# Attention and mixture-of-experts block: row order, a second gate bank, earlier scatters, later weight loads, one unused tile moved, and inner rows loaded by ScalarE

## The reference

```
xt = layernorm(x)                               # 2048 x 512
scores = softmax(xt @ Wg.T)                     # 16 experts
topi = 4 experts a token, out of the 2 best groups of 4
h = silu(xt @ W1[e].T) * (xt @ W3[e].T)         # 352 inner values, expert e
y = sum over the 4 experts of score * (h @ W2[e].T)
z = silu(xt @ Ws1.T) * (xt @ Ws3.T) @ Ws2.T     # shared part, 704 inner values
out = x + y + z
```

## Time and profile before

| | |
|---|---|
| time, median of 3 runs | 955.37 us (953.28 to 955.61) |
| profiled execution's own time | 954.32 us |
| its span | 952.7 us |
| PE busy | 914.0 us (96%) |
| DVE, ACT, POOL busy | 557.2, 332.3, 494.8 us |
| moved by DMA | 218.97 MB |

### The profile page before, as it was taken

The page is one execution under the profiler, slowest core; times in us unless marked ns, Lnnn a source line. Parts: engine busy times, 40 slices in busy tenths (PEclk is TensorE's granted clock), DMA queues, the critical chain, the costliest instruction groups (busy, mean ns, idle before and its releaser), DMA issues.

```text
span 952.7 us, 19359 instructions
## 1 busy us (share of the span) xinstructions
PE 914.0 (96%) x4962; PEld 811.7 (85%) x4963; DVE 557.2 (58%) x1103; ACT 332.3 (35%) x708; POOL 494.8 (52%) x346
## 2 busy tenths in 40 slices
PE   8999998899999996899999999999999999997998
PEld 5778876688889985899999999999999999896997
DVE  6656766898885542344444444444444444465997
ACT  4466553443334221233333333333333333321221
POOL 1137777772276675044644665456666634046771
PEclk9999999999999999899999999999999999998999
DMA  6739995664677767657785777777778755577884
GB/s 210 259 116 388 390 402 183 238 201 139 194 268 243 249 221 229 203 154 247 218 260 165 248 247 248 245 246 231 248 247 255 246 166 154 155 212 209 265 264 131
DMA packets 180649, 218.97 MB, mean 230 GB/s; under 512 B 56576, under 2 KB 124160, under 8 KB 180224
## 3 DMA queue, kind: packets, MB, share of 16 engines
q1 hardware_dynamic: 118080, 123.49, 40.4%
q0 software_dynamic: 20816, 79.44, 24.9%
q10 hardware_dynamic: 41712, 15.54, 6.0%
HBM read 127.38 MB, written 91.03 MB: 229 GB/s over the span
## 4 chain that ended last, share of the span: by engine, by line
PE 75%; DVE 9%; issue 5%; DMA 5%; ACT 3%; SPq 1%; POOL 1%; ACTq 0%; DVEq 0%; POOLq 0%
PE ps L1153 14%; PE ps L1154 14%; PE ps L1155 14%; PE ps L1205 8%; PE ps L1207 8%; PE ps L1206 8%; DMA hblk<-h_d 2%; PE ps L1008 2%; PE ps L1021 2%; DVE st L1450 1%; PE ps L955 1%; DVE res L1448 1%; SPq L408 1%; DMA xslot_d<-scat,sloti 1%; DVE st L1267 1%
## 5 line engine op out<-in xcount | busy, mean ns | idle before, releaser
L1153 PE MATMUL ps<-whi,xhi 128*128 (+1 forms) x888 | 291.3, 328 | 10.7 <-issue 8.6
L1154 PE MATMUL ps<-wlo,xhi 128*128 (+1 forms) x888 | 288.7, 325 | 0.0
L1155 PE MATMUL ps<-whi,xlo 128*128 (+1 forms) x888 | 288.6, 325 | 0.0
L1153 PEld LDWEIGHTS ps<-whi,xhi 128*128 128x128 f32 x888 | 169.3, 191 | 17.4 <-issue 12.7
L1525 DVE TENSOR_TENSOR hrow<-ps,sg 128x352 f32<-128x352 f32 x95 | 49.8, 524 | 224.6 <-ACT sg L827 224.4
L1154 PEld LDWEIGHTS ps<-wlo,xhi 128*128 128x128 f32 x888 | 169.5, 191 | 4.0
L1155 PEld LDWEIGHTS ps<-whi,xlo 128*128 128x128 f32 x888 | 169.0, 190 | 0.0
L827 ACT ACTIVATE sg<-ps 128x352 f32<-128x352 f32 x111 | 51.5, 464 | 283.9 <-PE ps L1155 283.9
L834 ACT ACTIVATE xhi<-ps 128x512 fp32r<-128x512 f32 x112 | 66.9, 597 | 150.7 <-DVE ps L1486 150.6
L560 POOL TENSOR_TENSOR wlo<-raw,whi 128x2816 fp32r<-128x2816 f32 x16 | 100.5, 6283 | 2.4 <-POOL whi L558 0.3
L654 POOL DMA_INDIRECT raw<-yslot_d,sloti x64 | 69.3, 1083 | 57.7 <-DMA yslot_d<-ysb 28.3
(11 more groups left out here) (199 smaller groups left out, 1597.7 us busy)
## 6 DMA issues: line engine op xcount, KB each, us to landing
raw<-wexp_in POOLq DMA_DIRECT2D x18, 2176.0 KB, 11.4
xslot_d<-zero SPq DMA_DIRECT2D x10, 2048.0 KB, 21.2
xg<-xslot_d SPq DMA_DIRECT2D x320, 64.0 KB, 2.1
yslot_d<-ysb SPq DMA_DIRECT2D x80, 256.0 KB, 2.2
h_d<-hrow ACTq DMA_DIRECT2D x79, 192.0 KB, 2.5
hblk<-h_d SPq DMA_DIRECT2D x79, 192.0 KB, 2.6
xg<-xn_d SPq DMA_DIRECT2D x128, 64.0 KB, 3.4
xq<-x_in SPq DMA_DIRECT2D x16, 256.0 KB, 3.4
```

Source lines behind the costliest of these rows:

```text
L1153: pe.matmul(ps[:, 2 + m, 0:INTER], xh, wh, start=(k == 0), stop=False)
L1154: pe.matmul(ps[:, 2 + m, 0:INTER], xh, wl, start=False, stop=False)
L1155: mm = pe.matmul(ps[:, 2 + m, 0:INTER], xl, wh, start=False, stop=(k == KT - 1))
```

## The change

Six things are changed, all in the second half.

1. Row order: DVE multiplies expert tile 0 (`first_row`) ahead of the last shared tile's addition instead of behind it.
2. Bank 7: an odd expert tile's gate half goes to bank 7. `up` of an expert tile starts its gate half when the silu of the tile two before is done, and waits for the tile before only ahead of the multiplier half.
3. Scatter: token tile t is scattered when `up` of tile t-1 is done, not of tile t+1 (both cut off at the ends).
4. Weight sets: the raw load of set o+1 is issued inside `split` of set o, once set o's own raw weights have landed, not right behind the split of set o-1.
5. Unused tile: the table that counts leading tiles is read two entries earlier, so there is one leading tile less (2 instead of 3 with these inputs) and one trailing tile more. The odd tiles get a count of their own for the first gather.
6. `load_h` goes from SP's program to ACT's, behind `store_h` of the tile after.

```diff
+        def gate_bank(base, p):
+            return 7 if base == NT and p else 2
...
-            def load_h(t, r, turn):
-                if type(t) is int and t == NR - 1:
-                    return
-                hold(sp, h_stored[r], 16 * (turn + 1))
-                if type(t) is not int or t >= XG:
-                    hold(sp, h_tr, NT + t - XG + 1)
-                sp.dma_start(hblk[:, r, :], h_d[r * P:(r + 1) * P, :]).then_inc(h_loaded[r], 16)
-
             sp.wait_ge(y_zeroed, 16 * (NR - NT * TOPK) // 8)
-            stream(sp, [(NR, True, [(-1, load_h), (XG + 1, load_slots), (-3, store_y)], None),
-                        (NT, False, [(0, None), (XG + 1, load_tile(NT + NR, xn_d)), (-4, store_out)], None)], XG)
+            stream(sp, [(NR, True, [(XG + 1, load_slots), (-3, store_y)], None),
+                        (NT, False, [(XG + 1, load_tile(NT + NR, xn_d)), (-4, store_out)], None)], XG)
...
                 hold(pool, raw_loaded[p], 16 * (half + 1))
+                if type(o) is not int or 2 < o < NW - 1:
+                    next_raw(o + 1, 1 - p)
                 hold(pool, mm1, 2 + before)
...
             def next_raw(o, p):
-                hold(pool, w13_ready, o + 1)
-                hold(pool, w2_ready, o + 1)
-                pool.dma_start(raw[:, p, :].rearrange("p (c n) -> p c n", c=PIECES), wexp[bass.ds(o + 2, 1), :, :, :].rearrange("a c p n -> p (a c) n")).then_inc(raw_loaded[p], 16)
+                hold(pool, w13_ready, o - 1)
+                hold(pool, w2_ready, o - 1)
+                pool.dma_start(raw[:, p, :].rearrange("p (c n) -> p c n", c=PIECES), wexp[bass.ds(o, 1), :, :, :].rearrange("a c p n -> p (a c) n")).then_inc(raw_loaded[p], 16)
...
-                pool.wait_ge(mm1, 2 + (min(t + 2, NT) if t else 1))
+                pool.wait_ge(mm1, 2 + max(t, 1))
...
-            def set_and_next(o, p, half):
-                split(o + 2, p, half + 1, tiles_through(o + 2))
-                if type(o) is int and o == 0:
-                    pool.wait_ge(first_lo, 2 * NT)
-                    load_weights(1, 3)
-                next_raw(o + 2, p)
-
-            pipeline(pool, NW - 4, [(0, set_and_next)])
-            for o in range(NW - 2, NW):
-                split(o, o % 2, o // 2, tiles_through(o))
+            def set_on(t, p, half):
+                split(t + 3, 1 - p, half + 1 + p, tiles_through(t + 3))
+
+            split(2, 0, 1, tiles_through(2))
+            pool.wait_ge(first_lo, 2 * NT)
+            load_weights(1, 3)
+            pipeline(pool, NW - 4, [(0, set_on)])
+            split(NW - 1, (NW - 1) % 2, (NW - 1) // 2, tiles_through(NW - 1))
 
 
             pool.wait_ge(w2_ready, NW)
-            stored = pool.value_load(order[0:1, NRP + E:NRP + E + 1], min_val=8 * NT * TOPK, max_val=16 * (NR // 2))
-            for p in range(2):
+            for p, at in enumerate((NRP + E, NTAB - 1)):
+                stored = pool.value_load(order[0:1, at:at + 1], min_val=8 * NT * TOPK, max_val=16 * (NR // 2))
                 hold(pool, y_stored[p], stored)
...
+            def load_h(t, r, turn):
+                if type(t) is int and t == NR - 1:
+                    return
+                hold(act, h_stored[r], 16 * (turn + 1))
+                if type(t) is not int or t >= XG:
+                    hold(act, h_tr, NT + t - XG + 1)
+                act.dma_start(hblk[:, r, :], h_d[r * P:(r + 1) * P, :]).then_inc(h_loaded[r], 16)
...
-            stream(act, [(NR, True, [(0, by_two(silu_g(NT))), (0, store_h), (-2, high_first), (2, by_two(x_high_e)), (-2, high_later), (-3, by_two(y_evac))], None),
...
+            stream(act, [(NR, True, [(0, by_two(silu_g(NT))), (0, store_h), (-1, load_h), (-2, high_first), (2, by_two(x_high_e)), (-2, high_later), (-3, by_two(y_evac))], None),
...
-                    two = base == NT and type(t) is int and t in (2, 3)
                     pe.wait_ge(x_lo, base + t + 1)
-                    if 1 in halves and not two:
+                    if base == NT:
+                        pe.wait_ge(silu, base + t - 1 if type(t) is not int or t else base)
+                    elif 1 in halves:
                         pe.wait_ge(h_ready, base + t)
                     else:
                         pe.wait_ge(silu, base + t)
@@ -1142,17 +1147,18 @@
                         return
                     pe.wait_ge(w13_ready, need)
                     for m in halves:
-                        if two and m:
+                        if base == NT and m:
                             pe.wait_ge(h_ready, base + t)
+                        bank = 3 if m else gate_bank(base, p)
...
-                            pe.matmul(ps[:, 2 + m, 0:INTER], xh, wh, start=(k == 0), stop=False)
-                            pe.matmul(ps[:, 2 + m, 0:INTER], xh, wl, start=False, stop=False)
-                            mm = pe.matmul(ps[:, 2 + m, 0:INTER], xl, wh, start=False, stop=(k == KT - 1))
+                            pe.matmul(ps[:, bank, 0:INTER], xh, wh, start=(k == 0), stop=False)
+                            pe.matmul(ps[:, bank, 0:INTER], xh, wl, start=False, stop=False)
+                            mm = pe.matmul(ps[:, bank, 0:INTER], xl, wh, start=False, stop=(k == KT - 1))
...
-                step(dve.tensor_scalar(total[:, 1, 0:NL], const[:, C_TILE + NT * TOPK + 1:C_TILE + NT * TOPK + 2 * NL:2], total[:, 0, 0:1], None, ALU.is_ge))
+                step(dve.tensor_scalar(total[:, 1, 0:NL], const[:, C_TILE + NT * TOPK - 1:C_TILE + NT * TOPK - 2 + 2 * NL:2], total[:, 0, 0:1], None, ALU.is_ge))
...
+                step(dve.tensor_scalar(ecmp[:, 0:NR // 2, 0], const[0:1, C_TILE + 1:C_TILE + NR:2], ntile[0:1, 0, E - 1:E], 16.0, ALU.is_lt, ALU.mult))
+                step(dve.tensor_reduce(tabf[:, NRP + E + 1 + NL:NTAB], ecmp[:, 0:NR // 2, 0], AX, ALU.add))
...
+            def first_row(t, r, turn):
+                if type(t) is int and t == NT - 1:
+                    h_row(NT)(0, 0, 0)
+
+            def later_rows(t, r, turn):
+                if type(t) is not int or t >= 1:
+                    h_row(NT)(t, r, turn)
+
+            pipeline(dve, NT, [(2, x_turn_on), (1, x_low_on), (0, h_mult_on), (0, route_1), (0, route_2), (-1, first_row), (-1, add_shared(0)), (0, h_low_on),
                                (0, second_set), (0, expert_rows)], ramp=11, ring=XG)
-            stream(dve, [(NR, True, [(0, h_row(NT)), (-2, turn_first), (-2, low_first), (2, x_turn_r), (-2, turn_later), (2, x_low_r), (-2, low_later),
+            stream(dve, [(NR, True, [(0, later_rows), (-2, turn_first), (-2, low_first), (2, x_turn_r), (-2, turn_later), (2, x_low_r), (-2, low_later),
```

More of the change, by code:

```diff
@@ L39 @@
 NRP = NR + 4
+NTAB = NRP + E + 1 + NL + 1
 PIECE = WCOL // NT
```

9 lines of the change are left out of this document (4 added, 5 removed).

## The result

| | before | after |
|---|---|---|
| median of the runs, us | 954.33 (951.97 to 955.61, 4 runs) | 941.78 (939.81 to 943.77, 4 runs) |
| profiled execution, us | 954.32 | 943.77 |
| its span, us | 952.7 | 942.2 |

The account below looks back on a forecast made before the run. PE's matmuls were taken to bound the experts at 5.97 us a tile, leaving only stalls to win: 954.3 - 12.7 (start) - 8.8 (end) + 2.5 (steady) = 935.3, or 936.4 on the median's side; 8-in-10 range 929.5 to 944.

Parts of the forecast that it names:

- Start: Shared stage to experts, 350 to 400 us: 17.7 us lost, 5 left, gain 12.7; bounds 1 and 12 left.
- The gate: Scatters released by an earlier up: they end near 343 instead of 353.8 and land 10.8 us earlier.
- the leading tile's cover: At the start, the first real tile is wanted 3.86 us sooner; the scatter's 10 us cover that cost.
- The 1.42 us at up 1: At the start, up 1 was 1.42 us late behind the first hrow; the wait goes, a shorter one comes before up 2.
- sets 3 and 4 no longer overlap: At the start, set 4's raw load leaves only when set 3's has landed, some 11.4 us later; argued against stalls staying.
- the loads out of SP's line: Inner row loads on ACT's queue save SP's place in line: at the start load 0 leaves near 358, not 365.95.
- End: First tiles of the last stage: gathers 11.9 us earlier, 9.3 us lost, 0.5 left, gain 8.8; bounds 9.4 and 4.
- The half microsecond that I left for heavier traffic: Last stage: 0.5 us of loss kept for heavier DMA traffic beside the last inner rows.
- Steady stretch: Amid the experts, later inner row loads cost 0.2 us at each of 13 raw loads, 2.5 us; bounds 0 and 20.
- the sentence on ACT's standing: Amid the experts, ACT stands until the store before lands, delaying xhi and hhi; up to 1 us of delay is absorbed.
- rival A: Steady stretch: ACT's store wait costs PE 2 to 3 us at each of 13 raw loads; 960 or more, chance 0.05.
- The move's own rule: Inner row loads on ACT's queue: same 16 DMA engines, so no landing gets shorter; only SP's place in line is saved.

Follow-up runs that it names:

- the undoing: Against the kernel with five parts and inner row loads on SP: three leading tiles and one count for both y stores again; 937.21 us, ratio 0.9892.
- the loads on SP: Changed kernel with only the inner rows' loads put back in SP's program, the five other parts kept; 928.79 us, ratio 0.9789.
- the late loads on SP: Five parts with inner row loads in SP's program, each load held until the next row is multiplied; 932.61 us, ratio 0.9811.
- the kernel that only stands: Against the kernel with held loads on SP: ACT also waits for the same store, without issuing anything; 940.38 us, ratio 0.9866.
- the move alone: Kernel before with only the inner rows' loads moved to ACT's queue; 965.19 us, ratio 1.0162.
- the full wait: Five parts, loads in SP's program, one bank, and from tile 4 on up waits for the whole row of the tile before; 932.00 us, ratio 0.9842.
- without bank 7: Five parts, loads in SP's program, both gate halves in bank 2 again; 927.22 us, ratio 0.9743.

## Why the prediction was right, and where not

**Start: right, with one wrong name in it.** 12.98 us measured, 12.7 forecast; with a scatter of up to 3 us there, so near a match is in part luck. The gate carries 7.8 of it, the leading tile's cover included. The 1.42 us at up 1 went too (silu 0 to 1 fell from 7.68 to 5.88), but I had put them down to the row's place in DVE's list; the old place costs nothing, and by elimination (it wasn't tried by itself) it was `up`'s wait for silu in place of the row. The new order of raw loads, from which I drew "sets 3 and 4 no longer overlap", and the loads out of SP's line, which I held to be a gain, are both within the noise. (The "five long rows" with 9.5 us of idle are four, 1.42, 2.40, 3.03 and 2.63; the timeline has two shorter ones besides, 0.76 and 1.48, and all six make the 11.8.)

**End: right.** 8.92 measured, 8.8 forecast, 8.96 by the undoing. The half microsecond that I left for heavier traffic is there, but it has another cause: silu 79 follows 78 by 10.15 us after and by 9.71 with the loads on SP, where the gathers are as early. It is the queue's, not the traffic's, and without it the end gave 9.35, all of the 9.3 that were lost.

**Steady stretch: the mis-sized term.** I took 0.2 us for each of 13 raw loads, 2.5 in all. It measured 16.3, or 1.25 each, near my upper bound of 20; the half wait, which I had at nothing, paid 4.8 of it back, and 11.5 is what the time shows against the 2.5: the 9.0 us by which the steady term was off are, less 0.3 at the start, 0.1 at the end and 0.1 outside the ruler, the 8.5 between 935.3 and the profiled 943.77. The step that failed is the sentence on ACT's standing: "PE wants those only after another down and up, so I see up to 1 us of delay absorbed". I had worked out when the load lands, looked for the cost there, and gave ACT's standing no length. The landing was priced well (0.2 us each; the late loads on SP cost 2.96 us, 0.23 each), so the term that was missing is the standing. It follows from the rows: a store that takes 8.6 us is still out 2.7 us after the next one's issue begins, 5.94 us behind it as at 447.66 and 453.60, and ACT has nothing to do in between but stand. Measured, it stood 47.8 / 13 = 3.7 us each time, where its usual wait for `xhi` is 114.0 / 56 = 2.0; of the difference a part was absorbed, and 0.9 (11.7 / 13, by the kernel that only stands) reached PE. That ACT is busy only a third of each step didn't help, since `hhi` and `xhi` come right behind the load. The row was there; I priced the queue and not what is queued behind it. The mechanism was rival A's; its price of 2 to 3 us each was too high except for one episode of 6, and its verdict (slower than before) held for the move alone: 1.0162. That the whole time stayed inside my range is luck: without the 4.8 us that I hadn't foreseen it would have been near 946.6, above 944.

**The half wait: missing from the sum.** "In the steady stretch PE has 0.5 us of idle in 340, so bank 7 is worth nothing there" was right of the bank and wrong of the wait. PE's busy time doesn't show such a delay: 339.49 of 340 us before, at 5.98 us a tile, and this row of the kernel with loads on SP, at 5.91:

```profile
480.00:820.00 340.00, 338.55 (x1889) 316.10 (x1888) 161.27 (x290) 112.32 (x232) 177.04 (x63) 1.00 0.72 225
```

Less busy, with more matmuls. The weight loads' busy time (PEld) goes the right way, 314.36 and 316.10, and 311.15 with the full wait. The Trainium skill (Perfetto Trace Analysis, Identifying the Most-Contended Engine) says just this, that matmul busy time is a poor measure because matmuls are pipelined, and that the share of weight loads serves better; the trace agrees. I took the mean of 5.97 us per tile for a floor, and the intervals tile by tile (5.9, 5.9, 6.0, 6.1) and PEld's row of 5.1 us would both have shown that it wasn't one.

**The move's own rule.** That the own queue makes no landing shorter held: the longest load took 11.7 us on ACT's queue and 9.4 on SP's, all other parts the same.

**The faster kernel.** The five parts with the loads on SP beat both: ratio 0.9789 against the changed kernel's 0.9871. These two intervals overlap a little (0.9860 and 0.9837), and it is the steady stretch, 413.70 against 430.02, that tells them apart. The ratio without bank 7 was lower still, 0.9743, but its steady stretch is the same 413.69 and the rest lies within what can't be told at the start; the two aren't told apart.

## What to carry to other kernels

A DMA that must wait for another's landing belongs on an engine with nothing urgent behind it: what counts is not how busy the engine is but what stands next in its list, and for how long the slowest landing, not the median, keeps it there. When a change bundles edits, undo them one by one, and measure by stage with an instruction that occurs once per tile; a time that fits the forecast can hide two wrong terms of opposite sign. And a share of busy time near 100% is no proof that a step is at its floor: look at the intervals, step by step.

## What the runs showed of the hardware

- A small store (192 KB) amid a raw load of 2.2 MB took up to 11.6 us to land where its median is 2.5, and a load up to 11.7 where it is 2.9 (changed kernel).
- ACT, made to wait in its own list for the landing of a store, 13 times and 49.5 us in all, lengthened the steady stretch by 11.72 us without issuing anything. SP waited for the same stores in a kernel where ACT didn't, and there the late loads cost 2.96 us.
- After an idle of 4.22 us PE's granted clock was 0.54 for the next 3.6 us (matmuls 0.43 us apart instead of 0.23), 1.2 GHz of its 2.4, and 0.99 in the 6 us after. After one of 1.81 us in the kernel where ACT only stands, it was 0.73 from 460 to 464 us and 0.89 in the 6 us after. PE's nine waits of 0.37 to 1.20 us between 480 and 820 us left the changed kernel's clock at 1.00.
- The steady stretch repeats to 0.01 us over 414 us in six kernels on three chips, one profiled execution each, while the whole time of one kernel moves by 1 to 7 us from run to run.
